# Expert stage of a perceiver layer: ScalarE gets its own copy of the second weights' scale and takes activation halves ahead of each gelu

## The reference

```python
logits = (x @ gate_w + gate_b) / TEMP
topk_vals, topk_idx = jax.lax.top_k(logits, 2)          # 2 of 8 experts
...
h = einsum('bsd,edf->bsef', x, w1) + b1                 # 512 -> 2048
h = gelu(h)
expert_out = einsum('bsef,efd->bsed', h, w2) + b2       # 2048 -> 512
out = einsum('bse,bsed->bsd', gate_probs, expert_out)   # then a layer norm
```

## Time and profile before

| what | value |
|---|---|
| median of three runs | 1486.8 us |
| the profiled execution: its own time | 1486.2 us |
| its span | 1484.6 us |
| TensorE matmul busy (PE) | 1343.7 us, 91% |
| VectorE busy (DVE) | 1027.9 us, 69% |
| ScalarE busy (ACT) | 874.3 us, 59% |
| span up to the expert jobs | 0 to 823 us |
| expert jobs | 823 to 1440 us |
| mixing, last layer norm, stores | 1440 to 1484.6 us |

### The profile page before, as it was taken

One profiled execution on the slowest core, in us unless ns is written; L12 is line 12 of the kernel. 1 busy time (PEld: TensorE's weight loads), 2 busy tenths in 40 slices (PEclk: granted clock), 3 DMA queues, 4 the chain that ended last, 5 costly groups with the idle time before them and its releaser, 6 DMA issues.

```text
span 1484.6 us, 26700 instructions
## 1 busy us (share of the span) xinstructions
PE 1343.7 (91%) x8412; PEld 865.1 (58%) x8413; DVE 1027.9 (69%) x2163; ACT 874.3 (59%) x1404; POOL 161.4 (11%) x200
## 2 busy tenths in 40 slices
PE   6879999999999999999987889989899898998977
PEld 5658677686776867768665444444444444444432
DVE  5655876868768687686766576666666667666665
ACT  3567776777767777677780455545555555555530
POOL 1001011020110201202012000000000000000014
PEclk9999999999999999999998999999999999999997
DMA  9696254262543625436168716605143346000015
GB/s 365 260 354 222 79 204 164 107 240 78 203 160 110 240 78 200 162 112 241 58 245 337 277 33 264 268 21 224 66 159 138 115 182 268 28 14 21 14 32 153
DMA packets 70482, 241.15 MB, mean 162 GB/s; under 512 B 5422, under 2 KB 5532, under 8 KB 64292
## 3 DMA queue, kind: packets, MB, share of 16 engines
q1 hardware_dynamic: 57232, 156.77, 29.6%
q0 software_dynamic: 13184, 83.89, 14.8%
q10 hardware_dynamic: 28, 0.01, 0.0%
HBM read 177.73 MB, written 62.91 MB: 162 GB/s over the span
## 4 chain that ended last, share of the span: by engine, by line
PE 50%; DVE 18%; issue 12%; ACT 10%; DVEq 3%; DMA 2%; POOL 2%; SPq 1%; ACTq 1%
PE bank L1629 8%; PE bank L1587 7%; PE bank L1550 4%; PE bank L1655 4%; DVE v_sb L592 4%; PE bank L1571 3%; ACT arena L455 3%; PE bank L724 2%; PE bank L726 2%; PE bank L725 2%; PE bank L1596 2%; DVE blocks L592 2%; DVE kqT L592 2%; PE bank L1611 2%; PE bank L1677 2%
## 5 line engine op out<-in xcount | busy, mean ns | idle before, releaser
L1587 PE MATMUL bank<-moe_w 128*128 128x257 f32 x768 | 190.1, 385 | 6.5 <-DVE moe_w L1006 6.5
L1587 PEld LDWEIGHTS bank<-moe_w 128*128 128x128 f32 x768 | 138.2, 192 | 25.7 <-DVE moe_w L1006 5.8
L585 DVE SCALAR_TENSOR_TENSOR arena<-bank,now_h,arena 128x512 f16<-128x512 f32 x92 | 69.1, 751 | 111.0 <-ACT arena L455 111.0
L704 PE MATMUL bank<-moe_w,arena 128*128 x368 | 141.0, 383 | 0.0
L705 PE MATMUL bank<-moe_w,arena 128*128 x368 | 140.4, 382 | 0.0
L706 PE MATMUL bank<-moe_w,arena 128*128 x368 | 139.6, 379 | 0.0
L462 ACT ACTIVATE y<-moe_w,now_v 128x1024 f16 x46 | 52.8, 1148 | 131.4 <-DVE now_h L565 90.9
L1629 PE MATMUL bank<-moe_w 128*128 128x512 f16 x384 | 114.4, 379 | 10.0 <-ACT moe_w L1063 7.0
L449 ACT ACTIVATE arena<-arena 128x512 f32<-128x512 f32 x92 | 57.9, 629 | 108.4 <-DVE arena L543 108.4
L462 ACT ACTIVATE wosT<-moe_w,now_v 128x1024 f16 x92 | 100.4, 1139 | 18.2 <-PE bank L726 18.2
L1049 ACT ACTIVATE moe_w<-bank,cols,ugain 128x512 f32<-128x512 f32 x96 | 74.6, 777 | 61.6 <-PE bank L1630 60.8
(11 more groups left out here) (282 smaller groups left out, 3095.2 us busy)
## 6 DMA issues: line engine op xcount, KB each, us to landing
moe_w<-in_L_ffn_w_dram SPq DMA_DIRECT2D x46, 1024.0 KB, 6.1
moe_w<-w_halves POOLq DMA_DIRECT2D x8, 4096.0 KB, 13.0
moe_w<-in_L_ffn_w_dram POOLq DMA_DIRECT2D x8, 4096.0 KB, 24.5
w_halves<-moe_w SPq DMA_DIRECT2D x48, 512.0 KB, 4.2
xs_rows<-blocks SPq DMA_DIRECT2D x8, 2048.0 KB, 15.3
arena<-in_ctx_dram SPq DMA_DIRECT2D x32, 384.0 KB
arena<-in_L_ffn_w_dram SPq DMA_DIRECT2D x10, 1024.0 KB, 5.1
blocks<-in_L_ffn_w_dram SPq DMA_DIRECT2D x8, 1024.0 KB, 4.9
```

Source lines behind the costliest of these rows:

```text
L704: nc.tensor.matmul(bank[fb % 2][:, :], xT_low[:, k, :], high, start=(k == 0), stop=False)
L1587: last = nc.tensor.matmul(bank[h][:, 0:KEYS], qkT[:, c, b, h * P:(h + 1) * P], cnT[:, b % 2, c, :], start=(c == 0), stop=(c == KC - 1))
```

## The change

`v_scale_act` is new on ScalarE: at the head of each job it copies the expert's scale of the second weights to a tile of its own, `now_v_act`, with an activation of 128x1, and waits for that instruction to end. All `v_hi` use this tile, so ScalarE needs VectorE's `now_v` no more. On VectorE the pair is taken apart: `now_h` is copied right after `h_lo(j-1, 3)`, and `now_v` after `v_lo(j-1, 3)`, where both stood. On ScalarE every `h_hi` now comes ahead of the gelu that it followed, and the wait for `now_h` stands before `h_hi(j, 0)`, behind `v_hi(j, 0)`.

```diff
                 for i in range(2):
                     nc.scalar.activation(v_high[fb % 2][i], moe_flat[:, bass.ds(slot * 16384 + 8192 + fb * 2048 + i * 1024, 1024)],
-                                         ACT.Identity, scale=now_v[:, 0:1]).then_inc(v_high_done, 1)
+                                         ACT.Identity, scale=now_v_act[:, 0:1]).then_inc(v_high_done, 1)
+
+            def v_scale_act(j, e):
+
+                if not isinstance(j, int) or j > 0:
+                    act.wait_ge(v_high_done, 2 * FB * j)
+                nc.scalar.activation(now_v_act[:, :], job_scales[:, bass.ds(e, 1), KD + 1], ACT.Identity).then_inc(now_v_act_ok, 1)
+                act.wait_ge(now_v_act_ok, j + 1)
 
             def job(j, first, last):
-                slot = act.value_load(job_e[0:1, bass.ds(j, 1)], min_val=0, max_val=EXPERTS - 1) % 2
-                gelu(j, 0)
+                e = act.value_load(job_e[0:1, bass.ds(j, 1)], min_val=0, max_val=EXPERTS - 1)
+                slot = e % 2
                 if not first:
                     h_hi(j - 1, 3)
+                v_scale_act(j, e)
+                gelu(j, 0)
+                v_hi(j, 0, slot)
                 act.wait_ge(now_h_ok, j + 1)
-                v_hi(j, 0, slot)
+                h_hi(j, 0)
                 gelu(j, 1)
-                h_hi(j, 0)
                 v_hi(j, 1, slot)
+                h_hi(j, 1)
                 gelu(j, 2)
-                h_hi(j, 1)
                 v_hi(j, 2, slot)
                 if not last:
                     x_hi(j + 1)
+                h_hi(j, 2)
                 gelu(j, 3)
-                h_hi(j, 2)
                 v_hi(j, 3, slot)
...
-            def h_scales_now(j, e):
+            def h_scale_now(j, e):
 
                 if not isinstance(j, int) or j > 0:
                     dve.wait_ge(hT_out, FB * j)
+                nc.vector.tensor_copy(now_h[:, :], job_scales[:, bass.ds(e, 1), KD + 2]).then_inc(now_h_ok, 1)
+
+            def v_scale_now(j, e):
+
+                if not isinstance(j, int) or j > 0:
                     dve.wait_ge(v_low_done, 2 * FB * j)
-                nc.vector.tensor_copy(now_v[:, :], job_scales[:, bass.ds(e, 1), KD + 1])
-                nc.vector.tensor_copy(now_h[:, :], job_scales[:, bass.ds(e, 1), KD + 2]).then_inc(now_h_ok, 1)
+                nc.vector.tensor_copy(now_v[:, :], job_scales[:, bass.ds(e, 1), KD + 1]).then_inc(now_v_ok, 1)
...
                 if not first:
                     h_lo(j - 1, 3)
+                h_scale_now(j, e)
+                if not first:
                     v_lo(j - 1, 3, slot_of(j - 1))
-                h_scales_now(j, e)
+                v_scale_now(j, e)
```

More of the change, by code:

```diff
@@ L256, in perceiver_layer @@
         job_scales = sb("job_scales", [P, EXPERTS, KD + 4])
+        now_v_act = sb("now_v_act", [P, 1])
         now_v, now_h, now_y, now_b = sb("now_v", [P, 1]), sb("now_h", [P, 1]), sb("now_y", [P, 1]), sb("now_b", [P, 1])
@@ L308, in perceiver_layer @@
         hT_high_done, v_high_done, v_low_done = sem("hT_high_done"), sem("v_high_done"), sem("v_low_done")
+        now_v_ok, now_v_act_ok = sem("now_v_ok"), sem("now_v_act_ok")
         now_h_ok, now_y_ok, now_b_ok = sem("now_h_ok"), sem("now_y_ok"), sem("now_b_ok")
@@ L591, in v_lo @@
                     dve.wait_ge(v_high_done, 2 * (FB * j + fb) + i + 1)
+                    if fb == 0 and i == 0:
+                        dve.wait_ge(now_v_ok, j + 1)
                     nc.vector.scalar_tensor_tensor(out=v_low[fb % 2][i], in0=moe_flat[:, bass.ds(slot * 16384 + 8192 + fb * 2048 + i * 1024, 1024)],
```

## The result

The changed kernel takes **1410.8 us** (median of four runs, 1407.6 to 1411.8) against 1487.9 for the kernel before, measured beside it: a ratio of 0.948, with a 95% interval of 0.946 to 0.950. The forecast was 1413, in a range from 1405 to 1428. The profiled execution has a span of 1406.0 us where the one before had 1484.6.

A forecast was written before the change was run, and what follows sets the result against it. TensorE's wait before mm2(j,0) and the clock's fall were taken as the bound; 66.9 (19 jobs) + 6.5 (first jobs) + 0.5 (before mm2(0,0)) = 73.9 us off 1486.2, plus 0.6 for the median: 1413 us, range 1405 to 1428.

The forecast's parts named there:

- The bound: TensorE, 91% busy: its idle time in the expert stage, 2.12 us before mm2(j,0) in every loop job.
- the two sizes of job: From one wait before mm2(j,0) to the next: 25.31 or 27.01 us; the 1.69 difference is the clock.
- the sum of 70.5 us lost in 19 jobs: mm2(3,0) to mm2(22,0): 505.95 us against 19 jobs of 22.92 us of TensorE work.
- h_hi ahead of gelu: On ScalarE: h_lo(j-1,3) at 4.06 us into a job instead of 5.20; h_lo(j,0) waits no more for h_hi(j,0).
- VectorE's copies: In a job on VectorE: now_h 0.90 us after h_lo, v_lo(j-1,3) 1.01 later, now_v at 8.60.
- ScalarE's own copy: Head of each job: 0.45 us with its wait, 3 us of cover; the 4.14 us wait before v_hi(j,0) goes.
- 0.5 us gained there: Before mm2(0,0): the wait shrinks by the 0.54 us between gelu and h_hi, counted as 0.5.
- The wait left: Before mm2(j,0): start at 14.46 us, due 14.27, so 0.19 us left, with VectorE's own chain as cause.
- The first three jobs: mm2(0,0) to mm2(3,0): 80.39 us, 11.6 more than three jobs of work; 6.5 taken as saved.
- The rivals: Longer VectorE chain 0.09, clock falls anyway 0.05, wait stays 0.03, slower as ScalarE's copy holds up gelu(j,0) 0.03.
- the longer chain: VectorE's chain longer than laid out, y_copy stays 1.0 us late: +15 us, 1428; chance 0.09.
- the fall of the clock: TensorE's clock falls all the same, 15 jobs go on paying 1.69 us: +25, 1438; chance 0.05.

The follow-up runs named there:

- The filled wait: Kernel before, with 16 matmuls of 256 columns, written where nobody reads, put between hT_fill(j,1) and mm2(j,0): 1461.3 us, 0.982.
- the kernel that waits nowhere: Changed kernel with VectorE's two copies together behind v_lo(j-1,3) again; ScalarE's own copy and its order stay: 1403.0 us, 0.943.
- The experiment with the late y_copy: Changed kernel with an unread maximum over 2048 columns on VectorE ahead of each y_copy from job 1 on: 1484.7 us, 0.998.

## Why the prediction was right, point by point

- *The bound, the two sizes of job and the sum of 70.5 us lost in 19 jobs*: right. The filled wait shows the clock's part alone (25.4 us in the 19 jobs), the kernel that waits nowhere the rest (22.90 us a job, laid out 22.92).
- *h_hi ahead of gelu*: right, and the main part; alone it gives 69 us.
- *VectorE's copies*: right to 0.02 us a step and 0.04 in all, up to y_copy. The page of the Trainium skill that was weighed ("VectorE: DVE Perf Modes", "The DRAIN you can't avoid") says that a semaphore after each operation costs nothing extra. Here the copy of now_h, which waits for the semaphore of h_lo, came 0.90 us after it and not 0.67.
- *ScalarE's own copy*: its price was mis-sized upwards (0.45 laid out, 0.31 measured with its wait) and hidden, as laid out. It ended the wait for now_h, which is worth 17 us on top of the new order. That it costs nothing was wrong in one place: in job 0 it pushed a table load of 1.28 us out of its cover. The prediction counted 0.5 us gained there, the trace has 1.0 lost. The 0.5 was mis-sized by itself: with only the order changed, mm1(0,0) to mm2(0,0) takes 11.30 us instead of 11.42, 0.1 gained.
- *The wait left*: 0.15 where 0.19 was laid out.
- *The first three jobs*: 8.4 us where 6.5 was taken, within the 3 to 10 given. Of the 8.4, 1.7 is a fall of the clock there that the prediction did not list (the granted clock was 0.50 from 882.6 to 886.0 us before). The three waits left there (0.95, 1.38 and 0.14 us) did not lower the clock.
- *The 3.7 us before mm1(0,0)* are not the change's. The code there is the same in all ten kernels, and mm1(0,0) starts between 819.9 and 823.6 us; the profile of before happens to be the latest of them, that of after the earliest.
- *The rivals*: none came. The experiment with the late y_copy forced the longer chain and the fall of the clock, and each cost what was laid out for it (2.19 us a job for the 2.20 put in, 1.69 a fall).

The forecast counted the parts together and did not ask what each is worth. Had it done so, it would have found the split of VectorE's pair to be a loss: the pair is not late for h_hi(j,0) once h_lo(j-1,3) comes sooner and ScalarE has its own copy (now_h at about 8 us, h_hi at 8.98).

## What to carry to other kernels

Lay a job out on all engines from one time zero, with start-to-start times; it shows which change of order is worth what, and the longest wait of an engine need not be the dearest one; here it was worth a quarter of what the order was. A copy that is split off to be early can cost more than it brings, when it bares something that a long instruction had covered. And price an idle time of TensorE with what follows it: here 2.1 us of waiting cost 3.8 in most jobs.

## What the runs showed of the hardware

- In 19 jobs of the kernel before, each with one wait of 2.12 to 2.15 us, TensorE's granted clock fell to the level of 1.2 GHz behind 15 of the waits; where the wait was brought back (2.18 to 2.21 us), behind 15 of 19 too. Each fall cost 1.69 us. 38 waits of 0.86 and 1.5 us in one kernel lowered it not once, nor did three of 1.60 to 1.68 in the kernel with only the order changed. The shortest wait of the expert jobs with a fall behind it was one of 1.99 us.
- The length of the wait alone does not decide it: in job 0 the clock fell behind 2.02 us in two kernels and not behind 2.09 in four. In the kernel before, the fall comes 0.2 us behind the wait's end in one job, then 0.5, 0.8, 1.1 and 1.3 in the next ones, and then a job goes free, so that four or five jobs pay and one doesn't. Why is not shown.
- Filling the idle time with matmuls whose results nobody reads kept the clock at 1.00 and saved 27 us.
- An instruction of VectorE with a read of the expert's number ahead of it started about 1 us after the instruction before (1.02 in both places shown), and 0.32 after it with the read moved away. Behind an instruction of 0.75 us the read shows as 0.27 us of issue, behind one of 0.15 as 0.87; at the head of a job, where it falls under v_lo's instructions of 1.28 us, no idle time shows.
- A table load of ScalarE can stand behind a wait of the activation that follows it. Here its 1.28 us then came after the wait, and hT_fill(0,0) 0.51 us and mm2(0,0) 1.0 us later.
